# Two-layer language tower with a routed expert layer: token numbers scattered instead of token rows, gathers spread, new orders of stages

## What is computed

```python
h = take(L0_tok_weight, x)                                  # 16 x 128 tokens, rows of 256
h = h + L0_attn(layernorm(h))                               # causal linear attention, 16 heads, per row of 128
h = h + L0_ffn(layernorm(h))                                # one 256x256 product, scaled
h = h + L1_attn(layernorm(h))                               # softmax-kernel attention, then relu feed-forward of 1024
h = h + L1_ffn(layernorm(h))                                # 8 experts, one per token, and a shared expert
# L1_ffn, for every token:
logits = x @ router_w.T; top = argmax(logits); score = sigmoid(max(logits))
h = silu(x*score @ gate[top]) * (x*score @ up[top]); moe = h @ down[top]
sh = silu(x @ shared_gate) * (x @ shared_up) @ shared_down  # width 512
return moe + sh
```

## Time and profile before

| | |
|---|---|
| median of three runs | 749.82 us |
| the profiled execution | 749.15 us |
| its span | 747.3 us |
| TensorE matmul busy | 679.7 us, 91% |
| VectorE busy | 481.6 us, 64% |
| ScalarE busy | 277.1 us, 37% |
| GpSimd busy | 204.1 us, 27% |
| DMA | 69.81 MB, of which 41.10 MB written to HBM |
| chain that ended last | TensorE 83%, VectorE 6%, issue 3% |

### The profile page before, as it was taken

One profiled execution on the slowest core, in us unless ns is written; L12 is line 12 of the kernel. 1 busy time (PEld: TensorE's weight loads), 2 busy tenths in 40 slices (PEclk: granted clock), 3 DMA queues, 4 the chain that ended last, 5 costly groups with the idle time before them and its releaser, 6 DMA issues.

```text
span 747.3 us, 15335 instructions
## 1 busy us (share of the span) xinstructions
PE 679.7 (91%) x5738; PEld 563.1 (75%) x5739; DVE 481.6 (64%) x1185; ACT 277.1 (37%) x664; POOL 204.1 (27%) x379
## 2 busy tenths in 40 slices
PE   3838899999999999999999999999997399999995
PEld 2627788988889898989989898888886256565653
DVE  2549688887969788797988879777663422323231
ACT  1114443544344444534444453453442022222220
POOL 4632233313232422323242232422321011111111
PEclk9869999999999999999999999999999699999998
DMA  7999999999999500000000000000015411211110
GB/s 257 323 230 173 168 190 168 177 147 180 166 162 217 210 1 16 16 1 16 1 15 5 13 15 2 15 1 16 16 57 223 138 34 56 64 45 64 63 57 17
DMA packets 30911, 69.81 MB, mean 93 GB/s; under 512 B 3323, under 2 KB 9600, under 8 KB 29440
## 3 DMA queue, kind: packets, MB, share of 16 engines
q1 hardware_dynamic: 27696, 60.53, 37.0%
q0 software_dynamic: 3152, 8.40, 3.8%
HBM read 28.74 MB, written 41.10 MB: 93 GB/s over the span
## 4 chain that ended last, share of the span: by engine, by line
PE 83%; DVE 6%; issue 3%; ACT 2%; POOL 2%; DMA 2%; POOLq 0%; SPq 0%; DVEq 0%; ACTq 0%
PE ps L1030 76%; PE ps L1035 5%; PE ps L1199 2%; DMA H<-table,idx_sb 2%; POOL H L371 2%; ACT qkA L635 1%; DVE stats L659 1%; ACT yTB L625 1%; PE ps L1329 0%; POOL rstd L391 0%; DVE S_sb L725 0%; DMA yA<-sorted_rows 0%; DVE mv L660 0%; DVE kmax L811 0%; PE ps L1170 0%
## 5 line engine op out<-in xcount | busy, mean ns | idle before, releaser
L1030 PEld LDWEIGHTS ps<-yTC,we 128*128 128x128 f32 x1024 | 120.6, 194 | 6.5 <-issue 5.0
L1030 PE MATMUL ps<-yTC,we 128*128 128x128 f32 x1024 | 124.8, 279 | 0.5 <-ACT yTC L579 0.5
L390 POOL TENSOR_TENSOR var_eps<-mv,ln_eps 128x1 f32<-128x1 f32 x112 | 23.9, 213 | 370.4 <-DVE mv L660 370.1
L1030 PE MATMUL ps<-we,yTA 128*128 128x256 f32 (+1 forms) x288 | 97.1, 469 | 1.7 <-ACT yTB L625 1.4
L1030 PEld LDWEIGHTS ps<-we,yTA 128*128 128x128 f32 x288 | 54.6, 200 | 26.0 <-issue 20.9
L1030 PE MATMUL ps<-we,yTB 128*128 128x256 f32 (+1 forms) x216 | 73.1, 469 | 0.7 <-DVE yTB L863 0.6
L391 POOL TENSOR_TENSOR rstd<-var_eps,pow_half 128x1 f32<-128x1 f32 x112 | 66.4, 593 | 8.8
L1030 PE MATMUL ps<-we,ffT 128*128 128x256 f32 x256 | 61.3, 383 | 0.0
L1030 PEld LDWEIGHTS ps<-we,yTB 128*128 128x128 f32 x216 | 38.7, 191 | 23.7 <-issue 21.0
L1030 PEld LDWEIGHTS ps<-we,ffT 128*128 128x128 f32 x256 | 47.2, 190 | 5.6
L472 POOL DMA_INDIRECT out<-tmpA,home x12 | 11.8, 985 | 127.3 <-DVE tmpA L1019 127.3
(11 more groups left out here) (197 smaller groups left out, 1315.2 us busy)
## 6 DMA issues: line engine op xcount, KB each, us to landing
sorted_rows<-pads SPq DMA_DIRECT2D x16, 2052.0 KB, 49.1
we<-w_experts SPq DMA_DIRECT2D x8, 1536.0 KB, 19.5
home<-sorted_rows SPq DMA_DIRECT2D x23, 128.5 KB, 2.1
we<-w_ff SPq DMA_DIRECT2D x2, 1024.0 KB
rows_sb<-rows SPq DMA_DIRECT2D x1, 1664.0 KB, 7.0
yA<-sorted_rows SPq DMA_DIRECT2D x12, 128.0 KB, 2.1
yB<-sorted_rows SPq DMA_DIRECT2D x11, 128.0 KB, 2.1
we<-w_qk SPq DMA_DIRECT2D x2, 512.0 KB, 4.1
```

What stands on the lines that cost most here:

```text
L390: link(pool.tensor_tensor(var_eps[:, k:k + 1], mv[:, k, 1:2], ln_eps[:], ALU.add))
L1030: return pe.matmul(o, a, b, start=start, stop=stop)
```

## The change

Only token numbers are scattered by slot now. x and home rows go to DRAM in token order (`x_rows`, `home_rows`, stages `x_out` and `home_out` on SyncE). The sorted list of numbers (`sorted_ids`, one word per slot) is read back by SyncE in 23 loads into `ids`; GpSimd fetches the tiles of x and of home rows with indirect DMAs by these numbers. The padding rows go; 137 words per partition of the number list are preset. The table is computed with fewer operations inside VectorE's steps, and its two results are announced separately. The last expert's weights are loaded in three parts, each when the shared weights under it are free. Gathers go out one per step, on four semaphores. The shared expert's stages `c_ga`, `c_up`, `c_dn` have lags 8, 9 and 10, the router `c_lo` has 8; six buffers `yTC2` carry its input. Every engine has a new order of stages, TensorE's lags run from 0 to 10, and most stages have another PSUM bank and other `after` waits. The diff, cut to its core (bank assignments and most `after` waits are left out):

```diff
...
-GATHERED_ALONE = 3
+AHEAD = 6
+GATHERS = 4
...
-        qkv0_loaded out0_loaded middle_loaded last_loaded weights_scaled before_ready
-        experts_loaded
+        x_rows = nc.dram_tensor("x_rows", [T * P, D], F32, kind="Internal").ap()
+        home_rows = nc.dram_tensor("home_rows", [T * P, D], F32, kind="Internal").ap()
+        sorted_ids = nc.dram_tensor("sorted_ids", [(E * SPAN + 1) * P, 1], U32, kind="Internal").ap()
...
                 sp.dma_start(dst, src).then_inc(S["last_loaded"], 16)
-            sp.wait_ge(S["pads_ready"], 2)
-            sp.dma_start(sorted_dram[E * SPAN * P:, :], pads[:]).then_inc(rows_cleared[0], 16)
-            regions = sorted_dram[0:E * SPAN * P, :].rearrange("(e n p) r -> n p e r", e=E, p=P)
-            for n in range(T):
-                sp.dma_start(regions[n], pads[:].unsqueeze(1).broadcast_to([P, E, ROW])
-                             ).then_inc(rows_cleared[cleared_with(n)], 16)
+            sp.wait_ge(S["zero_ready"], 5)
+            sp.dma_start(sorted_ids.rearrange("(p n) one -> p (n one)", p=P), nowhere[:]).then_inc(S["ids_cleared"], 16)
             def load_experts(first, last, done):
                 for e in range(first, last):
...
             load_experts(0, RESIDENT, "experts_loaded")
-            sp.wait_ge(S["ffn0_psum"], T)
-            sp.wait_ge(S["out1_psum"], T)
-            load_experts(RESIDENT, freed_by_b, "experts_loaded")
-            sp.wait_ge(S["ff2_psum"], 2 * T)
-            load_experts(freed_by_b, freed_by_ff, "experts_loaded")
-            sp.wait_ge(S["down_psum"], T)
-            load_experts(freed_by_ff, E, "experts_loaded")
-            def first_row(j):
...
+            def x_out(t):
+                sp.wait_ge(S["sent_ready"], t + 1)
+                sp.dma_start(x_rows[t * P:(t + 1) * P, :], send_x[:]).then_inc(S["x_kept"], 16)
+            def home_out(t):
+                sp.wait_ge(S["tile_done"], t + 1)
+                sp.dma_start(home_rows[t * P:(t + 1) * P, :], send_home[:]).then_inc(S["home_kept"], 16)
+            def free_b(t):
+                if t == T - 1:
+                    sp.wait_ge(S["ffn0_psum"], T)
+                    sp.wait_ge(S["out1_psum"], T)
+                    load_experts(RESIDENT, freed_by_b, "experts_loaded")
+            def free_ff(t):
+                if t == T - 1:
+                    sp.wait_ge(S["ff2_psum"], 2 * T)
+                    load_experts(freed_by_b, freed_by_ff, "experts_loaded")
+            last = we[:, freed_by_ff * EXPERT:E * EXPERT]
+            def free_part(name, a, b, done):
+                sp.wait_ge(S[name], T)
+                sp.dma_start(last[:, a:b], w_experts[E - 1][:, a:b]).then_inc(S[done], 16)
+            def free_ga(t):
+                if t == T - 1:
+                    free_part("gate_psum", GATE, UP, "experts_loaded")
+            def free_up(t):
+                if t == T - 1:
+                    free_part("up_psum", UP, DOWN, "experts_loaded")
+            def free_dn(t):
+                if t == T - 1:
+                    free_part("down_psum", DOWN, EXPERT, "last_down_loaded")
+            def load_ids(t):
+                if t < T - 1:
+                    return
+                sp.wait_ge(S["table_ready"], 1)
+                sp.wait_ge(S["ids_scattered"], 16 * T)
+                for j in range(SORTED_TILES):
                     sp.sem_inc(S["unused"], 1)
-                    load(s, first_row(j))
-            def load_next_home(i):
-                for s, j in tiles_of(i):
-                    sp.wait_ge(home_stored[s], i * 16)
-                    sp.sem_inc(S["unused"], 1)
-                    load_home(s, first_row(j))
-            load_next(1)
-            with sp.Fori(2, ROUNDS - 1) as i:
-                load_next(i)
-                load_next_home(i - 1)
-            load_next(ROUNDS - 1)
-            load_next_home(ROUNDS - 2)
-            load_next_home(ROUNDS - 1)
+                    first = sp.value_load(tile_row[0:1, j:j + 1], min_val=0, max_val=E * SPAN * P)
+                    sp.dma_start(ids[:, j:j + 1], sorted_ids[bass.ds(first, P), :]
+                                 ).then_inc(S["ids_loaded0" if j < MOE_SLOTS else "ids_loaded1"], 16)
...
+            run_steps([
+                (5, home_out), (3, x_out), (0, free_b), (1, free_ff), (3, free_ga), (3, load_ids), (3, free_up),
+                (4, free_dn),
+            ])
...
+            def gather(t):
+                pool.indirect_dma_start(out=H[:, t, :], out_offset=None, in_=table,
+                                        in_offset=bass.IndirectOffsetOnAxis(ap=idx_sb[:, t:t + 1], axis=0)
+                                        ).then_inc(gathered[t % GATHERS], 16)
+            pool.wait_ge(S["idx_loaded"], 16)
+            for t in range(GATHERS - 1):
+                gather(t)
             pool.memset(proj_sb[:], 0.0).then_inc(S["zero_ready"], 1)
...
+            def gat(t):
+                if t + GATHERS - 1 < T:
+                    pool.wait_ge(S["var0_ready"], t + 1)
+                    gather(t + GATHERS - 1)
             def pA(t):
                 if t == 0:
-                    for later in range(GATHERED_ALONE, T):
...
             def scat(t):
-                pool.wait_ge(rows_cleared[cleared_with(t)], 16 * (5, 6, T - 10)[cleared_with(t)])
-                pool.wait_ge(S["slot_ready"], t * 2 + 2)
-                pool.wait_ge(S["sent_ready"], t + 1)
-                pool.wait_ge(S["tile_done"], t + 1)
-                pool.indirect_dma_start(out=sorted_dram, in_=send[:], in_offset=None,
-                                        out_offset=bass.IndirectOffsetOnAxis(ap=slot_u[:], axis=0)
-                                        ).then_inc(S["scattered"], 16)
+                if t == 0:
+                    pool.wait_ge(S["ids_cleared"], 16)
+                pool.wait_ge(S["slot_ready"], t + 1)
+                pool.indirect_dma_start(out=sorted_ids, in_=tokens[:, t:t + 1], in_offset=None,
+                                        out_offset=bass.IndirectOffsetOnAxis(ap=slot_u[:, t:t + 1], axis=0)
+                                        ).then_inc(S["ids_scattered"], 16)
...
                     pool.wait_ge(S["ey_ready"], j + 1)
-                    pool.sem_inc(S["unused"], 1)
-                    pool.indirect_dma_start(out=tokens_out, in_=ey[s], in_offset=None,
...
+            pool.wait_ge(S["x_kept"], 16 * T)
+            fetch_x(0)
+            pool.wait_ge(S["ids_loaded1"], 16 * (SORTED_TILES - MOE_SLOTS))
+            fetch_x(1)
+            pool.wait_ge(S["home_kept"], 16 * T)
+            fetch_home(0)
+            for i in range(ROUNDS):
+                if i + 2 < ROUNDS:
+                    fetch_x(i + 2)
                 store(i)
-            store(ROUNDS - 1)
+                if i + 1 < ROUNDS:
+                    fetch_home(i + 1)
         @block.scalar
         def _(act):
-            act.wait_ge(S["zero_ready"], 4)
...
-                after(dve, "scattered", t * 16)
-                dve.tensor_copy(send[:, 2 * D:ROW].bitcast(U32), token[:]).then_inc(S["slot_ready"], 1)
-                dve.wait_ge(S["slot_ready"], t * 2 + 1)
-                link(dve.tensor_scalar(token[:], token[:], float(P), None, ALU.add))
-                dve.tensor_copy(slot_u[:], slot[:]).then_inc(S["slot_ready"], 1)
+                dve.tensor_copy(slot_u[:, t:t + 1], slot[:]).then_inc(S["slot_ready"], 1)
...
+            def table0(t):
+                if t < T - 1:
+                    return
+                link(dve.tensor_tensor(exceeds, base[:].unsqueeze(2).broadcast_to([P, E, T]), beyond[:], ALU.is_gt))
+                link(dve.tensor_reduce(need, exceeds, AX.X, ALU.add))
+                link(dve.tensor_tensor(summed, need.unsqueeze(1).broadcast_to([P, E, E]), up_to[:], ALU.mult))
+                link(dve.tensor_reduce(ends, summed, AX.X, ALU.add))
+            def table1(t):
+                if t < T - 1:
+                    return
+                link(dve.tensor_tensor(first_tile, ends, need, ALU.subtract))
+                link(dve.scalar_tensor_tensor(out=shift, in0=first_tile, scalar=float(-P), in1=start_row,
+                                              op0=ALU.mult, op1=ALU.add))
+                link(dve.tensor_tensor(ended, by_tile(ends), tiles, ALU.is_le))
+                link(dve.tensor_tensor(begun, by_tile(first_tile), tiles, ALU.is_le))
+                link(dve.tensor_tensor(begun, begun, ended, ALU.subtract))
+            def table2(t):
+                if t < T - 1:
+                    return
+                link(dve.scalar_tensor_tensor(out=rows_at, in0=tiles, scalar=float(P), in1=by_tile(shift),
+                                              op0=ALU.mult, op1=ALU.add))
+                link(dve.tensor_scalar(rows_at, rows_at, float(-E * SPAN * P), None, ALU.add))
+                link(dve.tensor_tensor(rows_at, begun, rows_at, ALU.mult))
+                link(dve.tensor_reduce(sums, rows_at, AX.X, ALU.add))
```

(48 more changed lines are left out.)

272 lines of the change are left out of this document (125 added, 147 removed).

## The result

The changed kernel takes 753.04 us (median of 20 runs, 748.27 to 754.6), the old one beside it 747.86 (744.78 to 753.85): ratio 1.0061, 95% interval 1.0044 to 1.0079. Forecast were 744.7 and "faster" as the likeliest. The profiled execution took 751.52, its span is 749.7 against 747.3. In a later session, where both were run again on one chip, the old kernel's median was 756.65 and the ratio 0.9987 (0.9949 to 1.0025). The old kernel varies more from session to session, and there from execution to execution (748.33 to 761.97 in ten runs on one chip), than the two kernels differ. So the new kernel was 0.6% slower in the first session, and in the later one no difference can be told. The ratios leave out executions in a slower state, which the old kernel's medians beside the experiments include, so a ratio is not exactly the quotient of two medians.

The account below looks back on a forecast made before the run. TensorE was taken to bound the pipeline's middle steps, with 52.8 us of the tower not work. Terms +0.6 - 13.1 - 3 - 8 - 6.1 + 24.0 + 0.5 = -5.1 gave 744.7 us, range 731 to 760.

Parts of the forecast that it names:

- Gathers, fill, drain: Before the last count: -13.1 for TensorE's hole at 36.1 to 49.2 waiting on gathers, -3 fill, -8 drain.
- the 23.4: TensorE time lost in the fill beside the gathers' hole; half put down to the slow clock and expected to stay.
- Start-up +0.6, shared expert -6.1, table 5.2: First normalisation +0.6; last count 6.1 earlier, five shared-expert groups moving behind it; hand-over's table takes 5.2.
- Slot number, 1.1: Hand-over: VectorE forms the last slot number 1.1 us after the last count.
- Scatter, "4.1 to land, no later": Hand-over: scatter of token numbers runs beside the table, 1 to issue and up to 4.1 to land.
- Lists, 23 x 1.17: Hand-over: SyncE's 23 list loads take 26.9; the last expert's up part behind them 0.4 to issue, 3.9 to land.
- Rival B: Lists cost only the accepted spacing of 0.53, row numbers being loaded ahead: 14.7 less, 730; chance 0.10.
- D: Rival: the lists are paid with their landing, one at a time, 23 x 2.28 = 52.4: 770.2; chance 0.06.
- Expert rounds +0.5: Expert rounds: matmuls unchanged, two more waits in TensorE's loop, +0.5 in all, bounds 0 and +2.
- C: Rival: VectorE bounds the partial steps, fill and drain give back nothing, pipeline four steps longer: +11, 755.7; chance 0.18.
- E: Rival: gathers land behind the weights and first four experts, up to the full 13.1 comes back: 757.8; chance 0.10.
- signs of being wrong: Middle steps longer than 32.6, lists at another spacing, or last count not 25 to 35 us earlier.

Follow-up runs that it names:

- experiment 8: Old kernel with only the gathers changed, 3 to 15 issued one a step on four semaphores: median 742.04 us, ratio 0.9793 to the old kernel.
- Experiment 1: Changed kernel with SyncE's two 1.5 MB expert loads issued at lag 3 instead of lag 1: median 746.13 us, ratio 0.9901 to the old kernel.
- Experiment 6: Changed kernel with token numbers scattered as rows of 512 bytes instead of 4: median 749.76 us, ratio 0.9945 to the old kernel.
- Experiment 2: Changed kernel with only 4 of the 23 token lists loaded before the last expert's up part, the others later: median 734.6 us, ratio 0.9744 to the old kernel.
- experiment 3: Changed kernel with TensorE's two new waits in the expert rounds kept only in round 0: median 751.92 us, ratio 0.9975 to the old kernel.
- experiment 7: Changed kernel with expert loads at lag 2, lists split, TensorE's two waits only in round 0, and 512-byte scatter rows: 726.07 us, ratio 0.9577 to the old kernel.
- experiment 9: Old kernel with 45 more GpSimd row gathers, five in each of nine expert rounds: span 764.9 us, ratio 1.0148 to the old kernel.
- experiment 5: Changed kernel with expert loads at lag 2, lists split, TensorE's two waits only in round 0: median 730.51 us, ratio 0.9703 to the old kernel.

## Why the prediction was wrong

It failed in the hand-over and the expert stage, by 15.1; the first stretch gave back 7.6 of it. That the time, 753.04, comes no further from 744.7 is luck: the losses alone would have led to 760, the upper end of the range, and nothing in the sum held the 7.6.

- **Gathers, fill, drain (-24.1 in all; measured -31.7).** The hole went as forecast. By experiment 8 the gathers alone are worth 15.6 (with the uncertainty said there), the 13.1 and most of the fill's 3. That leaves 16 for the new orders and the padding's end, where I had little more than the drain's 8; no run divides them. 3.1 of it lie in the middle, put at 0. In the kernel before, three of its steps took 33.48, 32.90 and 34.47 and the other seven 32.54 or 32.55; in the kernel after all six full steps take 32.52. So the new order's step is no shorter; the early loss went. It lay between 120 and 221 us, where the padding kept the transfer engines full (share 1.02), and experiment 8, with padding and old order, has it too (steps of 33.0 to 34.5). That points to the padding, but isn't shown: in the later executions of the new order, without padding, three of the six full steps took 32.85, and what that is stays open.
- **The fill's account.** The prediction put half of the 23.4, 11.7, down to the slow clock at the start. By its own row that clock, 0.87 over 26.4 us, is worth 3.4. The term was kept, so the sum doesn't suffer.
- **Start-up +0.6, shared expert -6.1, table 5.2.** The first transposition moved from 9.74 to 10.36; behind the last count come the five groups forecast; the table took 5.0.
- **Slot number, 1.1: measured 7.5.** The step that failed. I followed what stands behind the lists in SyncE's queue, but not what stands ahead of the new home transfers: the loads of lag 1 were at this place in the old kernel too, where no 128 KB transfer with a waiter came right behind them. Nor did I ask who waits for tile 12's home rows, only for tile 14's. Experiment 1: 6.9.
- **Scatter, "4.1 to land, no later": measured 7.1.** I took the landing of 2052-byte rows for 4-byte rows and argued from less data to less time. From the slot number to the first list it took 7.6 instead of the table's 5.2, so it cost 2.4. Experiment 6.
- **Lists, 23 x 1.17, and the up part behind them: 26.9 and 4.0, both right.** Experiment 2 shows that they, and not the rows, set the end. Rival B (spacing 0.53) and D (paid with their landing) are out: the issues are 1.12 apart as a rule and 1.16 on the mean. The fixed cost of about 2.0 us that the prediction took from the Trainium skill ("DMA: Bandwidth & Descriptors", Anatomy of one DMA) stands there for DMAs that GpSimd issues; SyncE's lists landed after 2.0 as well, one overlapping the next.
- **Expert rounds +0.5 (0 to +2): measured +7.1.** Nine rounds are 0.14 longer, the last two 0.1 and 0.2, 1.5 in all, by two waits already fulfilled (experiment 3). The first round is 1.0 longer, starting at a granted clock of 0.72 instead of 0.79; the idle time of 28.3 before it need not be the reason, since experiment 7's first round also started at 0.72, after 5.1. 3.8 are at the end, in GpSimd's closing, with 46 more indirect DMAs issued (experiment 9), which I didn't have in the sum at all; 0.8 are the granted clock of the last down matmuls, unexplained.
- **The rivals.** C (VectorE bound in the partial steps) gives 755.7, near the time measured, but its mechanism didn't occur: fill and drain gave back more than forecast, not nothing. E did not occur: the gathers were in time with the weights ahead of them.

The form of the forecast was right, a large gain ahead of the last count against a loss behind it. With the two so near each other, the unpriced 15 us turned the sign. Two of the prediction's own signs of being wrong showed as well: the last count came 37.2 us earlier (38.7 in the later session), where 25 to 35 was named, and the later executions have middle steps above 32.6.

## What to carry to other kernels

Before a small transfer is put on a queue, write down what stands ahead of it there at that moment and who waits for its landing; a move that only exchanges the order with a large load moves the collision to the next small one. What must be fetched before an engine can go on should be issued ahead of what is only needed rounds later: four of the 23 lists were needed, and splitting them was worth 20.9 us. When an edit bundles a gain with new costs, try the gain alone.

## What the runs showed of the hardware

- A DMA of 128 KB issued on SyncE's queue 2.2 us behind two loads of 1.5 MB landed after 12.8 us instead of 1.7 (experiment 1 took the 6.9 us of delay away); behind 33 MB, ScalarE waited 61 us for one. The Trainium skill ("DMA: Bandwidth & Descriptors", Queues, rings and completion order) has each transfer engine take the descriptors of one queue in their order, and the trace agrees. The scatter on GpSimd's own queue was held up too, 10.8 instead of 7.6 with rows of 4 bytes (experiment 5) and 7.0 instead of 2.3 with rows of 512 (experiment 7).
- A scatter of 128 rows of 4 bytes landed in 7.6 us, of 512 bytes in 2.6 (medians, experiment 6).
- From the last store to the end of the span it took 5.8 us with 55 indirect DMAs issued by GpSimd, 9.5 with 100 and 9.6 with 101: 0.08 us each, if it is their number and not the written-out rounds (experiment 9).
- Two waits already fulfilled, in TensorE's loop on the critical path, cost 0.14 us a round.
- Unchanged code took up to 6.4 us longer up to the last count from one execution to another (543.3 and 549.6, the kernel after's tower), 3.2 of it even on one chip; behind the last count two executions of each kernel agreed within 0.02.
